# GpSimd adds epsilon and makes ScalarE's shift in all layer norms of a decoder kernel, with another hand-written order and another table of constant matmuls

## The chip, the cores and the metric

The kernel runs on one core of one Trainium2 chip. Its engines are TensorE (PE in the profile, with its weight loads as PEld), VectorE (DVE), ScalarE (ACT), GpSimd (POOL) and SyncE (SP), which issues the DMAs. They run their own instruction streams and meet at semaphores. The metric is the device time of one execution in microseconds; lower is better.

## The reference

Four sequences of 512 tokens with 256 channels go through two decoder layers. Each of the six sublayers is added to its input and a layer norm follows it:

```python
def _layernorm(x, axis=-1, eps=1e-05):
    m = jnp.mean(x, axis=axis, keepdims=True)
    v = jnp.var(x, axis=axis, keepdims=True)
    return (x - m) / jnp.sqrt(v + eps)

x = _layernorm(x + _L0_attn_ref(x, ...))        # causal softmax attention
x = _layernorm(x + _L0_xattn_ref(x, ctx, ...))  # masked cross attention, with a norm of its own inside
x = _layernorm(x + _L0_ffn_ref(x, ...))         # three layers of +1/-1 weights
x = _layernorm(x + _L1_attn_ref(x, ...))        # performer: causal linear attention, 16 heads
x = _layernorm(x + _L1_xattn_ref(x, ctx, ...))  # mLSTM: gated attention, 8 heads, group norm
x = _layernorm(x + _L1_ffn_ref(x, ...))         # quantized: rounded tokens and weights, conv of 3 taps
```

## The kernel before

**Streams.** The four sequences go as two streams, a (`first`) and b (`second`), in two rounds (n = 0, 1). Each stream has its own tiles and four of the eight PSUM banks, and both share the engines. A sequence is four tiles of 128 tokens (t = 0 to 3); most steps handle a pair p of them. The stages are called self, cross, sign, perf, mlstm and quant in the code; the first four are the front half.

**The order.** For each engine there is one generator for each stream that yields the name of a section ("sign.xT0") before it issues it. `weave` runs them by the strings in `TURNS`: "a12 b1 a6" is twelve sections of stream a, one of b, six of a. So the order on each engine is written out by hand, and an engine that waits for one stream doesn't pass to the other. Stream b runs behind a by about half a round.

**Constant matmuls.** At the head of many PE sections stands `claim`. It waits until the PSUM bank is free, and then issues as many 128x512 bf16 matmuls of constants into it as `KEEP` has for "section stream round" (line 558), 162 in all at 71 places. The result is overwritten. Only after them does PE wait for the operands of the section's own work.

**The norm of a pair.** `stats` on VectorE takes bn_stats of both tiles (L1181), bn_aggr (L1184), and adds EPS to the variances into `rstd` (L1187), which signals `var_in`. `rstd` on GpSimd raises that to the power -0.5 (L2116) and signals `rstd_made`. `normalize` on VectorE then makes the shift -mean*rstd of the pair (L1193), signals `shift_made`, and subtracts and multiplies the even tile (L1196). `normalize` on ScalarE waits for `shift_made` and makes the odd tile as rstd*x + shift (L1789). What follows, transposes on PE (L565) for instance, waits for both tiles. There are 56 such pairs; 8 of them are of the norm inside cross attention (i = 1), which has no shift and no ScalarE tile: there `spread_by_gamma` reads the mean and `add_residual` the rstd. At the very end the last normalized tiles are stored.

Line 1742 is the last scaling in quant (eight of 0.69 us to a pass), 2200 GpSimd's power in the mLSTM's group norm, 572 the projections, 1090 the taps of the convolution, 807 and 821 the performer's features, 1053 and 1042 the mLSTM's outputs.

## Time and profile before

| | |
|---|---|
| median of 3 runs | 794.84 us (794.0 to 796.28) |
| the profiled execution, its own time | 796.56 us |
| its span from the first to the last instruction | 795.2 us |
| outside the span | 1.36 us |
| instructions | 14785 |
| busy PE, DVE, ACT, POOL | 737.0, 572.7, 330.0, 183.3 us |
| granted TensorE clock, mean over the span | 0.985 |
| constant matmuls (L558) | 162 |

The profiled execution is 1.72 us above the median of the runs. Durations below come from it. A matmul's busy time overlaps that of the one behind it, since they are pipelined, so PE time is read as the distance from start to start: four constant matmuls take 0.88 us from the first start to the start of what follows, 0.22 us each.

### The profile page before, as it was taken

The numbers are of one execution on the slowest core, as the hardware profiler recorded it, in microseconds if no ns is written. First come the engines' busy times: TensorE is split into PE (matmuls) and PEld (weight loads), VectorE is DVE, ScalarE is ACT, GpSimd is POOL, SyncE is SP. The second block draws the span as 40 slices with busy tenths as digits, with TensorE's granted clock in tenths as the row PEclk, the third lists the DMA queues.
The fourth block names the chain that finished last, engine by engine and source line by source line (L and its number), as shares of the span: only waits on it lengthen the run. The fifth ranks groups of instructions, "written<-read, shape, count | busy, mean of one in ns | idle before, by whom it ended". The sixth has DMA issues, their size and how long they took to land.

```text
span 795.2 us, 14785 instructions
## 1 busy us (share of the span) xinstructions
PE 737.0 (93%) x5962; PEld 478.7 (60%) x5962; DVE 572.7 (72%) x1388; ACT 330.0 (42%) x608; POOL 183.3 (23%) x277
## 2 busy tenths in 40 slices
PE   9999999999999988899989999999999998998494
PEld 5778455667657655567654475857646585646232
DVE  1558745576476788988998963857656578799886
ACT  2576313323153226475338534241333413286253
POOL 8711000610015320022441020112204412012300
PEclk9999999999999999999999999999999999999698
DMA  9503000100011000041100030000000000000001
GB/s 349 194 2 133 0 1 1 54 2 2 1 28 28 27 2 2 1 120 42 27 2 1 0 107 1 2 1 3 1 1 1 1 2 2 1 2 1 0 1 53
DMA packets 12739, 23.76 MB, mean 30 GB/s; under 512 B 768, under 2 KB 7040, under 8 KB 12416
## 3 DMA queue, kind: packets, MB, share of 16 engines
q1 hardware_dynamic: 12672, 22.82, 8.3%
q8 instruction: 47, 0.77, 0.4%
q14 instruction: 20, 0.16, 0.1%
HBM read 20.72 MB, written 2.10 MB: 29 GB/s over the span
## 4 chain that ended last, share of the span: by engine, by line
PE 65%; DVE 18%; issue 8%; ACT 7%; POOL 2%; DVEq 0%; ACTq 0%; POOLq 0%
PE bank L762 8%; PE bank L580 6%; PE bank L572 6%; PE bank L627 5%; PE bank L606 4%; PE bank L856 4%; PE bank L772 3%; PE bank L1090 3%; PE bank L748 2%; PE bank L841 2%; PE bank L807 2%; DVE work L1474 2%; PE bank L866 1%; DVE stats L1181 1%; PE bank L710 1%
## 5 line engine op out<-in xcount | busy, mean ns | idle before, releaser
L2116 POOL TENSOR_TENSOR rstd<-rstd,minus_half 128x2 f32<-128x2 f32 x56 | 41.9, 748 | 434.3 <-DVE rstd L1187 434.0
L762 PE MATMUL bank<-work,f0w 128*128 128x512 f16 x512 | 114.2, 379 | 0.0
L762 PEld LDWEIGHTS bank<-work,f0w 128*128 128x128 f16 x512 | 49.4, 98 | 59.5 <-issue 1.9
L1904 ACT ACTIVATE work<-bank 128x512 f16<-128x512 f32 x64 | 37.1, 595 | 68.8 <-PE bank L762 47.7
L1392 DVE SCALAR_TENSOR_TENSOR work<-bank,work 128x512 f16<-128x512 f32 x64 | 43.0, 686 | 22.2 <-ACT work L1904 22.1
L558 PE MATMUL bank<-bar_upper,identb 128*128 128x512 bf16 x162 | 48.0, 389 | 4.9 <-DVE work L1474 2.0
L627 PE MATMUL bank<-work 128*128 128x256 f32 x208 | 50.6, 382 | 0.5 <-ACT work L1833 0.5
L1474 DVE TENSOR_TENSOR work<-bank,upper 128x512 f32<-128x512 f32 x64 | 41.3, 685 | 12.3 <-PE bank L856 12.0
L627 PEld LDWEIGHTS bank<-work 128*128 128x128 f32 x208 | 37.3, 190 | 5.8 <-ACT work L1833 1.0
L1257 DVE TENSOR_REDUCE small<-bank 128x1 f32<-128x512 f32 (+3 forms) x32 | 18.8, 587 | 30.0 <-PE bank L608 30.0
L2200 POOL TENSOR_TENSOR small<-small,minus_half 128x16 f32<-128x16 f32 x8 | 24.0, 3004 | 63.8 <-DVE small L1632 63.8
L856 PE MATMUL bank<-work 64*128 64x128 f32 x512 | 37.2, 285 | 1.6 <-DVE work L1456 0.9
L1181 DVE BATCH_NORM_STATS2 stats<-y 128x6 f32<-128x256 f32 x96 | 36.2, 414 | 3.0 <-ACT y L1882 2.9
L856 PEld LDWEIGHTS bank<-work 64*128 64x128 f32 x512 | 31.1, 187 | 11.2 <-issue 4.6
L572 PE MATMUL bank<-xT,perf_w 128*128 128x512 f32 x64 | 30.9, 615 | 1.5 <-ACT work L1929 0.6
L1929 ACT ACTIVATE work<-bank 128x512 f32<-128x512 f32 x40 | 21.2, 596 | 26.4 <-PE bank L807 26.4
L1818 ACT ACTIVATE work<-bank,small 128x512 f32<-128x512 f32 (+3 forms) x32 | 19.4, 606 | 27.4 <-DVE small L1261 19.8
L606 PE MATMUL bank<-ctxT,work 128*128 128x512 f32 x64 | 30.6, 600 | 0.0
L1090 PE MATMUL bank<-work,f0w 128*128 128x512 f32 x64 | 30.2, 595 | 0.4 <-DVE work L1695 0.4
L1569 DVE TENSOR_TENSOR work<-work 128x512 f32<-128x512 f32 x32 | 24.5, 787 | 6.6 <-ACT work L1990 6.3
L772 PE MATMUL bank<-f0w,work 128*128 128x256 f16 x256 | 29.3, 273 | 0.0
L558 PEld LDWEIGHTS bank<-bar_upper,identb 128*128 128x128 bf16 x162 | 15.0, 101 | 21.9 <-issue 5.2
(306 smaller groups left out, 1654.9 us busy)
## 6 DMA issues: line engine op xcount, KB each, us to landing
work<-in_mask SPq DMA_DIRECT2D x4, 1024.0 KB, 7.0
xT<-in_xT SPq DMA_DIRECT2D x4, 512.0 KB, 4.2
ctxT<-in_ctxT SPq DMA_DIRECT2D x4, 512.0 KB, 5.7
perf_w<-in_k SPq DMA_DIRECT2D x3, 512.0 KB, 11.7
perf_w<-in_perf_w SPq DMA_DIRECT2D x1, 1536.0 KB, 6.1
x<-in_x SPq DMA_DIRECT2D x2, 512.0 KB, 11.0
ctx<-in_w SPq DMA_DIRECT2D x2, 512.0 KB, 13.8
work<-in_w SPq DMA_DIRECT2D x1, 1024.0 KB, 16.1
```

Of the source, the lines that this page charges most:

```text
L558: nc.tensor.matmul(u.bank[:, :], identb[:, :], bar_upper[:, :, :].rearrange("p a b -> p (a b)"), start=True, stop=True)
L572: ins = nc.tensor.matmul(u.bank[:, :], weights[:, k, c0:c0 + P], src[:, k, :], start=(k == 0), stop=(k == NC - 1))
L580: ins = nc.tensor.matmul(u.bank[:, j * C:(j + 1) * C], src[:, k, t * P:(t + 1) * P], weights[:, k, c0:c0 + C], start=(k == 0), stop=(k == ...
L606: nc.tensor.matmul(u.bank[:, 0:width], s.a_qT[:, k, t * P:(t + 1) * P], keys[:, k, 0:width], start=(k == 0), stop=False)
L627: ins = nc.tensor.matmul(u.bank[:, 0:C], s.probT[:, t % 2, j * P:(j + 1) * P], v[:, j, :], start=(j == 0), stop=(j == tiles - 1))
L762: ins = nc.tensor.matmul(u.bank[:, :], f0w1[:, k, m * P:(m + 1) * P], s.h1[part][:, k, :], start=(k == 0 and part == 0), stop=(k == NF - 1 ...
L772: ins = nc.tensor.matmul(u.bank[:, 0:C], s.h2[part][:, k, t * P:(t + 1) * P], f0w2[:, k, :], start=(k == 0 and part == 0), stop=(k == NF - ...
L856: ins = nc.tensor.matmul(u.bank[:, here], s.kf[rows, pair, here], s.qf[rows, pair, here], start=True, stop=True, tile_position=(PM * i, 0))
L1090: ins = nc.tensor.matmul(u.bank[:, :], taps[:, j, k, :], s.flat[j % 4][:, k:k + T], start=(k == 0), stop=(k == 1))
L1181: m = vec.mark(nc.vector.bn_stats(s.stats[:, t, :], src[:, t, :]))
L1392: low_part(what, m, dst, number + m, lambda o, x, hi: nc.vector.scalar_tensor_tensor(out=o, in0=x, scalar=0.0, in1=hi, op0=ALU.max, op1=AL ...
L1474: nc.vector.tensor_tensor(s.inner[:, r % 4, :].rearrange("p (t q) -> p t q", t=NT), u.bank[:, :].rearrange("p (t q) -> p t q", t=NT), uppe ...
```

## The change

1. VectorE no longer adds EPS. The second bn_aggr signals `var_in` itself, and VectorE doesn't wait for the aggregates any more. GpSimd adds EPS from `mv` into `rstd`, waits for that, and takes the power.
2. VectorE no longer makes the shift. GpSimd makes it after the power, for the odd tile alone (one column), and signals `shift_made`; not in the norm i = 1.
3. `spread_by_gamma`, which relied on the wait that is gone, waits for `var_in`.
4. `TURNS` is another order on PE, DVE, ACT and POOL (SP's is the same), and `KEEP` is another table: 126 constants at 61 places.

```diff
 TURNS = {
     "tensor":
-        "a12 b1 a6 b1 a1 b1 a1 b1 a13 b4 a1 b3 p1 a2 b4 a3 b1 a7 b1 a19 b1 a2 b1 a2 b1 a1 b1 a1 b2 a1 b1 a1 b2 a1 b3 "
...
+        "a11 b1 a7 b1 a2 b2 a8 b1 a5 b4 a1 b4 p1 a2 b2 a3 b1 a5 b1 a11 b1 a5 b1 a4 b2 a1 b1 a2 b2 a1 b1 a1 b1 a1 b1 "
...
 KEEP = {
-    "quant.hidden5 0 0": 4, "quant.hidden6 0 0": 4, "quant.topT 0 0": 4, "quant.row2 0 0": 4, "self.q 0 1": 1,
...
+    "quant.turn0 0 0": 1, "quant.hidden1 0 0": 1, "quant.hidden3 0 0": 1, "quant.hidden4 0 0": 3,
...
         def stats(s, n, i, src, ready, p, name):
...
             dve.wait_ge(*m)
-            for t in (2 * p, 2 * p + 1):
-                m = vec.mark(nc.vector.bn_aggr(s.mv[:, t, :], s.stats[:, t, :]))
-            dve.wait_ge(*m)
-            two = slice(2 * p, 2 * p + 2)
-            nc.vector.tensor_scalar(s.rstd[:, two], s.mv[:, two, 1], EPS, None, ALU.add).then_inc(s.var_in.sem, 1)
+            vec.mark(nc.vector.bn_aggr(s.mv[:, 2 * p, :], s.stats[:, 2 * p, :]))
+            nc.vector.bn_aggr(s.mv[:, 2 * p + 1, :], s.stats[:, 2 * p + 1, :]).then_inc(s.var_in.sem, 1)

         def normalize(s, n, i, src, dst, p, name):
...
             dve.wait_ge(*s.rstd_made.at(n, s.place[i, p]))
-            nc.vector.scalar_tensor_tensor(out=s.shift[:, two], in0=s.mv[:, two, 0], scalar=-1.0, in1=s.rstd[:, two],
-                                           op0=ALU.mult, op1=ALU.mult).then_inc(s.shift_made.sem, 1)
             t = 2 * p
...
             def spread_by_gamma(p):

                 yield f"cross.in_norm{p}"
+                dve.wait_ge(*s.var_in.at(n, s.place[1, p]))
...
             yield f"{name}rstd{p}"
             pool.wait_ge(*s.var_in.at(n, s.place[i, p]))
             two = slice(2 * p, 2 * p + 2)
+            m = gps.mark(nc.gpsimd.tensor_scalar(s.rstd[:, two], s.mv[:, two, 1], EPS, None, ALU.add))
+            pool.wait_ge(*m)
             nc.gpsimd.tensor_tensor(s.rstd[:, two], s.rstd[:, two], minus_half[:, 0:2], ALU.pow).then_inc(s.rstd_made.sem, 1)
+            if i != 1:
+                pool.wait_ge(*s.rstd_made.at(n, s.place[i, p]))
+                t = 2 * p + 1
+                nc.gpsimd.tensor_scalar(s.shift[:, t:t + 1], s.mv[:, t, 0:1], -1.0, s.rstd[:, t:t + 1], ALU.mult,
+                                        ALU.mult).then_inc(s.shift_made.sem, 1)
```

Line numbers of the changed kernel are 2 lower than before up to `stats`, 7 and then 6 lower behind it, and 1 higher behind `rstd` on GpSimd. In the rows that follow, stretches of the program as they stand before and now are shown, without times.

**Place A: GpSimd, near the end, stream b's mLSTM.** Before: the six weighings of keys, the two powers of the group norm, and the powers of the two norm pairs; then the edges of the convolution.

```order
L2120 TENSOR_TENSOR ctx<-ctx,rows_all 128x256 x4
L2193 TENSOR_TENSOR work<-x,small 128x256 x6
L2200 TENSOR_TENSOR small<-small,minus_half 128x16 x2
L2116 TENSOR_TENSOR rstd<-rstd,minus_half 128x2 x2
L2206 MEMSET work 128x1
```

Now:

```order
L2121 TENSOR_TENSOR ctx<-ctx,rows_all 128x256 x4
L2194 TENSOR_TENSOR work<-x,small 128x256 x6
L2201 TENSOR_TENSOR small<-small,minus_half 128x16 x2
L2110 TENSOR_SCALAR rstd<-mv 128x2
L2112 TENSOR_TENSOR rstd<-rstd,minus_half 128x2
L2116 TENSOR_SCALAR shift<-mv,rstd 128x1
```

Each norm's power now has the addition ahead of it and the shift behind it (the second pair's three follow in the same way); the order of the rest is the same.

**Place B: VectorE, the same norm (its second pair).** L1742 (now L1736) is a scaling of stream a's quant, L1196 (now L1189) the even tile of the norm, L1663 (now L1657) the search for each token's largest value, which waits for both tiles. Before:

```order
L1181 BN_STATS stats<-y 128x6 x2
L1184 BN_AGGR mv<-stats 128x2 x2
L1187 TENSOR_SCALAR rstd<-mv 128x2
L1742 TENSOR_TENSOR work<-work,bank 128x512
L1193 SCALAR_TENSOR_TENSOR shift<-mv,rstd 128x2
L1196 TENSOR_SCALAR ctx<-y,mv,rstd 128x256
L1663 TENSOR_REDUCE small<-ctx 128x2
```

Now:

```order
L1179 BN_STATS stats<-y 128x6 x2
L1181 BN_AGGR mv<-stats 128x2
L1182 BN_AGGR mv<-stats 128x2
L1736 TENSOR_TENSOR work<-work,bank 128x512 x2
L1189 TENSOR_SCALAR ctx<-y,mv,rstd 128x256
L1657 TENSOR_REDUCE small<-ctx 128x2
```

The addition and the shift are gone, and between the aggregates and the even tile stand two scalings of the other stream in place of one. Ahead of the mLSTM's ratios, further up in the program, four of those scalings stand now, five before.

**Place C: TensorE, second round, stream b's second half of the performer features** (L807 queries and keys, L821 keys turned; 805 and 819 now) **beside stream a's mLSTM outputs** (L1042 and L1053; 1040 and 1051 now). L558 (now L556) are the constants. Before:

```order
L925 MATMUL bank<-work,head_spread 128x128 x4
L558 MATMUL bank<-bar_upper,identb 128x512 x4
L807 MATMUL bank<-work,perf_w 128x512 x4
L558 MATMUL bank<-bar_upper,identb 128x512 x4
L807 MATMUL bank<-work,perf_w 128x512 x4
L558 MATMUL bank<-bar_upper,identb 128x512 x4
L821 MATMUL bank<-perf_w,work 128x128 x12
```

Now:

```order
L805 MATMUL bank<-work,perf_w 128x512 x4
L556 MATMUL bank<-bar_upper,identb 128x512
L1040 MATMUL bank<-work,xT 128x132 x2
L556 MATMUL bank<-bar_upper,identb 128x512
L1051 MATMUL bank<-memory_back,work 128x132 x2
L1040 MATMUL bank<-work,xT 128x132 x2
L805 MATMUL bank<-work,perf_w 128x512 x4
L556 MATMUL bank<-bar_upper,identb 128x512 x2
L1051 MATMUL bank<-memory_back,work 128x132 x2
L819 MATMUL bank<-perf_w,work 128x128 x12
```

The same features have four constants ahead of and between them in place of twelve, and work of the other stream stands there.

## Rows read from the trace of the kernel before

**Rows 1.** The page: busy time by engine; the granted clock in 40 slices.

```profile
PE 737.0 (93%) x5962; PEld 478.7 (60%) x5962; DVE 572.7 (72%) x1388; ACT 330.0 (42%) x608; POOL 183.3 (23%) x277
...
PEclk9999999999999999999999999999999999999698
```

**Rows 2.** The page: the chain that ended last, by engine.

```profile
PE 65%; DVE 18%; issue 8%; ACT 7%; POOL 2%; DVEq 0%; ACTq 0%; POOLq 0%
```

**Rows 3.** Busy time by stretch: length, then each engine with instructions; clock; DMA; GB/s.

```profile
265.00:300.00 35.00, 30.02 (x368) 18.99 (x366) 29.85 (x74) 8.90 (x16) 12.04 (x21) 1.00 0.05 16
300.00:345.00 45.00, 38.48 (x426) 24.59 (x429) 42.64 (x85) 25.49 (x43) 4.17 (x6) 1.00 0.02 3
```

**Rows 4.** Groups of instructions: busy us, mean ns; idle before, what ended it.

```profile
L558 PE MATMUL bank<-bar_upper,identb 128*128 128x512 bf16 x162 | 48.0, 389 | 4.9 <-DVE work L1474 2.0 <-ACT work L1929 1.7 <-ACT work L1925 1.1
...
L1193 DVE SCALAR_TENSOR_TENSOR shift<-mv,rstd 128x2 f32<-128x2 f32 x48 | 12.1, 252 | 14.3 <-POOL rstd L2116 14.1
L1187 DVE TENSOR_SCALAR rstd<-mv 128x2 f32<-128x2 f32 x56 | 10.1, 180 | 1.9
...
L2116 POOL TENSOR_TENSOR rstd<-rstd,minus_half 128x2 f32<-128x2 f32 x56 | 41.9, 748 | 434.3 <-DVE rstd L1187 434.0
```

**Rows 5.** Timeline of PE: start, us, engine, line; constants and what follows them.

```profile
38.21 0.38 PE L558 MATMUL bank<-bar_upper,identb 128*128 128x512 bf16 x1
38.42 0.49 PE L565 MATMUL bank<-ident,x 128*128 128x128 f32 x3
...
722.34 0.59 PE L558 MATMUL bank<-bar_upper,identb 128*128 128x512 bf16 x2
722.77 0.38 PE L1001 MATMUL bank<-parts,head_row 128*128 128x512 bf16 x1
```

**Rows 6.** Timeline of PE at place C; in brackets idle before, what ended it.

```profile
656.39 1.03 PE L558 MATMUL bank<-bar_upper,identb 128*128 128x512 bf16 x4
...
660.12 1.04 PE L558 MATMUL bank<-bar_upper,identb 128*128 128x512 bf16 x4 [1.02 <-ACT work L1929]
...
662.92 1.04 PE L558 MATMUL bank<-bar_upper,identb 128*128 128x512 bf16 x4 [0.64 <-ACT work L1929]
```

**Rows 7.** Timeline of a norm pair that nothing delays (sign, stream a, first round).

```profile
117.78 0.25 DVE L1184 BATCH_NORM_AGGREGATE mv<-stats 128x2 f32<-128x6 f32 x2
118.06 0.17 DVE L1187 TENSOR_SCALAR rstd<-mv 128x2 f32<-128x2 f32 x1
...
118.31 0.69 POOL L2116 TENSOR_TENSOR rstd<-rstd,minus_half 128x2 f32<-128x2 f32 x1 [26.51 <-DVE rstd L1187]
...
119.04 0.16 DVE L1193 SCALAR_TENSOR_TENSOR shift<-mv,rstd 128x2 f32<-128x2 f32 x1 [0.25 <-POOL rstd L2116]
119.24 0.60 ACT L1789 ACTIVATE x<-y,shift,rstd 128x256 f32<-128x256 f32 x1 [5.64 <-DVE shift L1193]
```

**Rows 8.** Small instructions on GpSimd: two groups, and one in the timeline.

```profile
L2135 POOL TENSOR_SCALAR small<-small 128x32 f32<-128x32 f32 x4 | 1.6, 409 | 0.3
...
L2206 POOL MEMSET work<- 128x1 f32 x16 | 1.2, 98 | 2.7 <-DVE ctx L1196 1.6 <-DVE x L1196 1.1
...
145.82 0.30 POOL L2135 TENSOR_SCALAR small<-small 128x32 f32<-128x32 f32 x1
```

**Rows 9.** Timeline of a norm pair whose VectorE part comes late (cross, stream b).

```profile
161.90 0.70 POOL L2116 TENSOR_TENSOR rstd<-rstd,minus_half 128x2 f32<-128x2 f32 x1 [6.54 <-DVE rstd L1187]
...
165.59 0.60 ACT L1789 ACTIVATE x<-y,shift,rstd 128x256 f32<-128x256 f32 x1 [1.84 <-DVE shift L1193]
```

**Rows 10.** Timeline: a GpSimd addition and a VectorE shift at the same time.

```profile
415.51 1.28 POOL L2132 TENSOR_TENSOR work<-x 128x512 f32<-128x512 f32 x1
...
415.52 1.29 DVE L1193 SCALAR_TENSOR_TENSOR shift<-mv,rstd 128x2 f32<-128x2 f32 x1 [0.22 <-POOL rstd L2116]
```

**Rows 11.** Timeline of GpSimd at place A: the group norm's power and the next.

```profile
740.46 3.29 POOL L2200 TENSOR_TENSOR small<-small,minus_half 128x16 f32<-128x16 f32 x1 [1.03 <-DVE small L1632]
...
743.71 0.69 POOL L2116 TENSOR_TENSOR rstd<-rstd,minus_half 128x2 f32<-128x2 f32 x1
```

More of the change, by code:

```diff
@@ L38 @@
     "tensor":
[8 rows of a table removed]
-    "vector":
[11 rows of a table removed]
-    "scalar":
[6 rows of a table removed]
[8 rows of a table added]
+    "vector":
[11 rows of a table added]
+    "scalar":
[7 rows of a table added]
     "gpsimd":
-        "a7 b2 a5 b1 a1 b4 a5 b3 a1 b1 a2 b2 a2 b4 a2 b1 a2 b4 a3 b1 a4 b1 a2 b1 a1 b1 a1 b1 a1 b6 a2 b1 a1 b1 w1 b2 "
-        "a1 b1 a4 b1 a1 b9 a2 b2",
+        "a7 b2 a5 b4 a1 b1 a5 b5 a3 b1 a1 b1 a1 b3 a2 b1 a2 b5 a10 b2 a1 b5 a1 b2 a2 b3 w1 b3 a3 b1 a4 b9 a2 b2",
     "sync":
```

75 rows, old and new, of tables (KEEP, TURNS) are left out of this document.

## The prediction, made before the changed kernel had run

> **What bounds the kernel now.** I read the page first. TensorE is busy for 93% of the span, and its granted clock is the upper of its two levels, 2.4 GHz, nearly everywhere; the one slice marked 6 lies near the end, at 736 to 755 us [rows 1]. The chain that ended last is PE for 65% and VectorE for 18%, with 2% for GpSimd [rows 2]. So TensorE is the bound over most of the program, and VectorE shares that place in some stretches: from 265 to 345 us it is busy for 72.5 of 80 us, more than PE's 68.5 [rows 3]. But 162 of PE's matmuls are constants [rows 4] that compute nothing. At 0.22 us from start to start they hold 35 us of its time. They stand ahead of a wait, and whether they cost anything depends on whether the wait outlasts them. I went through the 71 places in the timeline. At 28 of them, with 54 constants, the work behind starts 0.21 to 0.23 us after the last constant's start and without idle time, as at the first and the last of them [rows 5]: no wait is left there, and in the worst case all of it is lost. At the other 43 a wait is still seen behind or ahead of them, and the constants mostly fill time that would be idle anyway. The 56 norm pairs lie between: each holds up only its own stream, and PE mostly has the other stream's work meanwhile.
>
> **The norm pair.** Today a pair with nothing in its way takes, from the end of the second aggregate (117.78 + 0.25) to the start of ScalarE's tile (119.24), 1.21 us: 0.03 to the addition, 0.17 for it, 0.08 to GpSimd, 0.70 for the power, 0.03 to the shift, 0.16 for it, 0.04 to ScalarE [rows 7]. The changed pair is 0.08 to GpSimd, the addition, a wait on itself, 0.70, a wait on itself, the shift, 0.04. The wait between two dependent GpSimd instructions is 0.3 us over four, so 0.08 [rows 8]. An addition over 2 columns on GpSimd is nowhere in the trace. From below it is bounded by a memset of one column, 0.10 us, and from above by the tensor_scalar over 32 columns, 0.30 us in an undisturbed place and 0.41 in the mean of four [rows 8]. I take 0.22 for it and for the shift: the instruction is of the kind of the dearer row, and its size is that of the cheaper one. That makes 0.08 + 0.22 + 0.08 + 0.70 + 0.08 + 0.22 + 0.04 = 1.42 us, 0.21 more than today. With 0.10 it is 1.18 (0.03 less), with 0.41 it is 1.80 (0.59 more). Moving small work to GpSimd doesn't shorten the chain in itself.
>
> It does so where VectorE is late. At 161.90 the power took 0.70 us and ended at 162.60, but ScalarE's tile started at 165.59 [rows 9], since the shift stood in VectorE's queue behind other work. 23 of the 48 shifts begin over 0.3 us after their power. There ScalarE gets free to start before VectorE's own tile, and the pair ends with VectorE's tile of 0.41 us, not with the shift, the hop and ScalarE's 0.60: about 0.38 us earlier. PE stands at the result of a norm pair at about a dozen of the 48, prompt and late ones mixed. Six times +0.21 and six times -0.38 is -1.0 us. Against that stand the last norms, which nothing covers. In the mLSTM near the end GpSimd ends the group norm's power at 743.75 and goes to the next at once [rows 11]; the addition, which VectorE made meanwhile, now comes behind it: +0.30. The last pair before the store is prompt: +0.21. At place B two scalings of 0.69 stand before the even tile in place of one, though one fewer stands ahead of the ratios, which evens out; and the rest of the mLSTM's and quant's prompt pairs in that stretch add about 1 us. I put the whole at **+0.5 us**, and between -2 and +9 (below).
>
> **What VectorE gets back.** The additions are busy for 10.1 us and the shifts for 12.1 [rows 4], 22.2 in all. The shifts' mean of 0.252 against 0.16 when prompt is contention: one took 1.29 us exactly beside a GpSimd addition of 1.28 us [rows 10]. The Trainium skill (GPSIMD Engine Reference, section 8, Key points) says that GpSimd shares its SBUF interfaces with VectorE, and that they contend when the VectorE instruction has two SBUF inputs; the rows agree, and by it the shift loses this stall when GpSimd itself makes it. The 22.2 us count only where VectorE is the bound: 0 if nowhere, 18% of them, 4.0 us, if by its share of the chain [rows 2]. I take the stretch of rows 3: 4 of the 56 pairs lie in it, so 22.2 x 4 / 56 = **-1.6 us**. The new wait in `spread_by_gamma` is on an aggregate right ahead of it, and it takes the place of the wait for the addition: nothing.
>
> **What PE gets back.** The table has 36 constants fewer, 7.9 us at 0.22. By place: the 28 places without a wait go from 54 to 27, 5.9 us less of paid time. The 43 others go from 108 to 59, and 40 constants stand at 25 new places. What the new ones cost is not known. If, as before, a third of them (54 of 162) is paid in full, they take 40 / 3 x 0.22 = 2.9 us. Ends: 8.8 if all are paid, 0 if all fill waits. Net **-3.0 us**. Of the covering ones that go, place C is where something better comes in. There twelve constants stand in three groups with 1.02 and 0.64 us of idle time ahead of two of them [rows 6], and now the other stream's mLSTM outputs stand there, with four constants. The eight that go are real work's time: **-1.8 us**, between 0 and the 1.8 + 1.66 of constants and idle time together. At the other covering places idle time takes the constants' place, at no cost, unless the clock falls. All groups there are of at most four, so 0.9 us, and idle time of that length was there before at full clock (1.02 us in rows 6); I count nothing.
>
> **Sum.** +0.5 - 1.6 - 3.0 - 1.8 = -5.9 us. Made against the profiled execution, that is 796.56 - 5.9 = 790.7 (795.2 of span before, 1.36 around it). That execution was 1.72 above the median, so the median of runs would be 794.84 - 5.9 = **788.9 us**. SP's order is untouched, and the DMAs before the last store are hidden.
>
> **Rivals.**
> *The waits stay (same).* PE's place is set by VectorE and ScalarE at the covering places, so fewer constants only become idle time; all 40 new ones are paid (8.8), against 5.9 that goes: +2.9. Place C gives 1.8, VectorE 1.6, and the norms cost 0.5: 794.8 us. For it speaks that at 43 of 71 places a wait outlasts the constants. Against it: the order was changed with the table, and waits move too.
> *More comes back.* The new constants all fill waits (-5.9), place C -1.8, VectorE by its share of the chain -4.0, norms at +0.5: -11.2, 783.6 us. For it speaks that VectorE is busier than PE for 80 us; against it, that GpSimd adds nothing to a prompt chain.
> *GpSimd's chain is the new bound (slower).* If both small instructions take 0.41 us, the mean with contention in rows 8, every prompt pair gets 0.59 us longer. The sign turns the sign once the pairs on the path number over 6.4 / 0.59 = 11, with -1.6 - 3.0 - 1.8 = -6.4 standing against them. With 16 on the path, in the chains of rounds' ends and of quant, it is +9.4 - 6.4 = +3.0, 797.8 us, and with the additions behind long GpSimd work (3.29 us in rows 11) up to 800. For it: 25 of 48 pairs are prompt today, and GpSimd's queue gets 104 more instructions, with a VectorE instruction of two inputs able to hold each up. Against it: PE has the other stream's work at most of them. The Trainium skill (GPSIMD Engine Reference, section 3.1, Elementwise) has the same direction: VectorE stays the engine for elementwise work. No row here shows a pair made in the new way.
> *The change doesn't free VectorE.* Two aggregates take 0.25 us, one about 0.17 [rows 7], so small instructions already overlap, and the freed slots may hold little; and if GpSimd's 104 new instructions stall VectorE as its addition did in rows 10, -1.6 becomes +1 or so, 791.5 us, inside the forecast's own range.
>
> **How the numbers follow.** Forecast 0.44 (own range 785.5 to 792.4), waits stay 0.17, more comes back 0.13, slower 0.23, not freed 0.03. A measurement of this kernel can tell about 0.3% from no change, which is 792.5 to 797.2. Faster: 0.44 + 0.13 + 0.03 = 0.60. Same is the case of the waits, 0.17. Slower is 0.23. The range 782.5 to 799 takes in all cases' centres, the unknown price of the small instructions and of the new constants, and leaves out the low tail of one and the high tail of the other, some 15%.
>
> **What would show it.** Steps right: L556 counts 126, and the start-to-start sum of constants falls from 35 to about 27 us; few constants directly followed by work without idle; GpSimd's addition and shift at 0.2 to 0.25 us in the median; a prompt pair at 1.4 us from aggregate to ScalarE's tile; VectorE's busy time down by some 20 us; place C without idle ahead of L805 and L819; the stretch that is now 265 to 345 us shorter by 2 us or more. Wrong: small GpSimd instructions of 0.4 us and more, PE idle at the transposes (L563, L1069) growing by several us, the granted clock falling at a place where constants are gone, or a longer stretch from stream b's last gate to the end, which takes 96 us now.

## The result, and the profile after

| | before | after |
|---|---|---|
| median of runs | 795.88 us (7 runs, 794.0 to 796.88) | 791.44 us (7 runs, 790.51 to 792.93) |
| ratio, 95% interval | | 0.9948 (0.9934 to 0.9962) |
| the profiled execution | 796.56 us, span 795.2 | 790.51 us, span 789.2 |
| busy PE, DVE, ACT, POOL | 737.0, 572.7, 330.0, 183.3 us | 728.3, 550.6, 330.8, 218.7 us |
| constants, from start to start | 162, 35.6 us | 126, 27.6 us |

The change makes the kernel 0.5% faster, 4.1 us (3.0 to 5.2), where 5.9 were forecast. The two profiled executions differ by 6.0 us, but that of before is one of its slower ones and that of after its fastest, so the traces overstate the gain by 1.9 us. Differences in us below are ratios times 795.

The page of after, its busy times and its granted clock; [rows 1] has those of before:

```profile
PE 728.3 (92%) x5926; PEld 476.3 (60%) x5926; DVE 550.6 (70%) x1284; ACT 330.8 (42%) x608; POOL 218.7 (28%) x381
...
PEclk9999999999999999999999999999999999999796
```

The groups that answer to [rows 4]. L2110 is GpSimd's new addition, L2116 its shift:

```profile
L2110 POOL TENSOR_SCALAR rstd<-mv 128x2 f32<-128x2 f32 x56 | 14.9, 267 | 397.1 <-DVE mv L1182 396.5
...
L556 PE MATMUL bank<-bar_upper,identb 128*128 128x512 bf16 x126 | 38.3, 389 | 5.2 <-DVE work L1468 2.5 <-ACT work L1919 1.4 <-ACT work L1923 0.6
L2112 POOL TENSOR_TENSOR rstd<-rstd,minus_half 128x2 f32<-128x2 f32 x56 | 40.5, 722 | 4.7
L2116 POOL TENSOR_SCALAR shift<-mv,rstd 128x1 f32<-128x1 f32 x48 | 17.2, 358 | 5.1
```

The timeline of the pair of [rows 7] in after, all three engines, and last the shift of the next pair:

```profile
122.48 0.18 DVE L1181 BATCH_NORM_AGGREGATE mv<-stats 128x2 f32<-128x6 f32 x1
122.58 0.15 DVE L1182 BATCH_NORM_AGGREGATE mv<-stats 128x2 f32<-128x6 f32 x1
...
122.81 0.22 POOL L2110 TENSOR_SCALAR rstd<-mv 128x2 f32<-128x2 f32 x1 [31.15 <-DVE mv L1182]
123.11 0.71 POOL L2112 TENSOR_TENSOR rstd<-rstd,minus_half 128x2 f32<-128x2 f32 x1
123.86 0.41 DVE L1189 TENSOR_SCALAR x<-y,mv,rstd 128x256 f32<-128x256 f32 x1 [0.76 <-POOL rstd L2112]
123.93 0.39 POOL L2116 TENSOR_SCALAR shift<-mv,rstd 128x1 f32<-128x1 f32 x1
...
124.36 0.60 ACT L1783 ACTIVATE x<-y,shift,rstd 128x256 f32<-128x256 f32 x1 [6.26 <-POOL shift L2116]
...
126.83 0.26 POOL L2116 TENSOR_SCALAR shift<-mv,rstd 128x1 f32<-128x1 f32 x1
```

From the end of the second aggregate (122.73) to ScalarE's tile (124.36) are 1.63 us, against 1.21. The addition takes the 0.22 us of the forecast. The shift takes 0.39 us here and 0.26 at 126.83, and the rows tell why: here VectorE's even tile runs from 123.86 to 124.27, and the shift ends 0.05 us behind it; there VectorE is idle. Of the 48 shifts 33 overlap the even tile. The 30 that begin behind its start took 0.39 to 0.43 us, and the 3 that begin ahead of it 0.26; of the 15 that don't overlap it 13 took 0.26. The freed VectorE now starts its tile just when GpSimd wants to make the shift. The Trainium skill (SBUF — State Buffer, Who interferes with whom) lists VectorE's `tensor_scalar` among the instructions that can enter a mode that takes the port pair shared with GpSimd, and says that the second to come then waits for the first to end. The order of starts agrees (0.39 us behind the tile, 0.26 ahead of it); which mode the tile ran in, no row shows.

**Where the time went.** I added up TensorE's own work (every matmul but the constants, each at the median distance to the next of its kind) and read when both kernels had done the same amount. The table has a row where the difference turns:

| own work done, us | before at | after at | difference |
|---|---|---|---|
| 20 | 25.2 | 24.5 | -0.7 |
| 40 | 46.1 | 47.6 | +1.5 |
| 200 | 229.5 | 231.6 | +2.1 |
| 280 | 359.4 | 358.4 | -1.0 |
| 360 | 453.5 | 451.5 | -2.0 |
| 480 | 592.9 | 588.4 | -4.5 |
| 520 | 642.3 | 638.8 | -3.5 |
| 540 | 683.9 | 677.2 | -6.7 |
| 560 | 710.3 | 702.7 | -7.6 |
| all | 795.2 | 789.2 | -6.0 |

Three places stand out: a loss of 2.2 us at 40 us, a gain of 3.1 between 230 and 359 us, and one of 3.2 at place C (638.8 to 677.2). The two orders do different work at the same amount, so a single row can be off by some us; at place C the rows of the two traces below give the same 3.2. Two more differences, a gain of 2.5 us between 453 and 593 us and a loss of 1.6 behind 710 us, no row here explains.

The loss is this, PE in after, and the granted clock there (by stretch: length; busy us and instructions of PE, PEld, DVE, ACT, POOL; clock; DMA; GB/s):

```profile
38.16 0.63 PE L563 MATMUL bank<-ident,x 128*128 128x128 f32 x4 [1.26 <-ACT x L1783]
38.63 5.30 PE L578 MATMUL bank<-wv,xT 128*128 128x256 f32 x16
...
36.00:40.00 4.00, 2.74 (x19) 2.49 (x19) 1.91 (x7) 2.58 (x3) 2.24 (x6) 0.94 0.00 0
40.00:44.00 4.00, 4.00 (x14) 3.24 (x13) 2.06 (x10) 3.25 (x8) 0.27 (x1) 0.63 0.01 2
```

In before [rows 5] the transposes at 38.42 followed their one constant without a wait. Here PE waits 1.26 us for ScalarE's tile of the first norm pair, and at 39.52 its clock falls to 1.2 GHz for 3.41 us; the 16 matmuls behind take 5.30 us, where before they took 3.62. In both kernels GpSimd comes to this pair only at 35.8 us, when its long work at the start ends. In before the power alone was left to it and ScalarE's tile began at 36.77; now the addition and the slower shift are too, and it begins at 37.42.

Before had such a fall as well, in the second round, and the prediction didn't see it: behind a wait of 0.81 us, also at transposes of normalized tiles, its clock is at the lower level for 3.41 us from 614.76.

```profile
613.83 0.63 PE L565 MATMUL bank<-ident,ctx 128*128 128x128 f32 x4 [0.81 <-DVE ctx L1196]
...
612.00:616.00 4.00, 3.08 (x26) 2.12 (x26) 2.99 (x9) 2.36 (x6) 4.00 (x8) 0.85 0.02 4
```

Place C in after, PE; [rows 6] show it before:

```profile
648.51 1.14 PE L805 MATMUL bank<-work,perf_w 32*128 32x512 f32 x8 [0.50 <-DVE y L1482]
649.59 0.39 PE L556 MATMUL bank<-bar_upper,identb 128*128 128x512 bf16 x1
...
650.26 0.38 PE L556 MATMUL bank<-bar_upper,identb 128*128 128x512 bf16 x1
...
651.69 1.14 PE L805 MATMUL bank<-work,perf_w 32*128 32x512 f32 x8 [0.15 <-issue]
652.77 0.60 PE L556 MATMUL bank<-bar_upper,identb 128*128 128x512 bf16 x2
...
654.34 0.95 PE L819 MATMUL bank<-perf_w,work 32*128 32x128 f32 x24 [0.52 <-DVE work L1435]
```

Idle time and constants come to 0.50 + 0.22 + 0.22 + 0.15 + 0.44 + 0.52 = 2.1 us. Before they were 1.57 from 656.39 to the first projection, 1.02 + 1.02 ahead of the second and 0.64 + 0.97 ahead of the turned keys, 5.2 us: 3.2 less.

### The profile page after: what moved, and what is told of

Read it like the earlier page. It is cut to its first block, busy times and chain, and to the rows that moved or that the text cites. A ratio compares the mean times of both kernels' runs of the same rounds, so it can differ in the third digit from the quotient of the medians.

```text
span 789.2 us, 14720 instructions
## 1 busy us (share of the span) xinstructions
PE 728.3 (92%) x5926; PEld 476.3 (60%) x5926; DVE 550.6 (70%) x1284; ACT 330.8 (42%) x608; POOL 218.7 (28%) x381
## 4 chain that ended last, share of the span: by engine, by line
PE 30%; DVE 10%; ACT 4%; POOL 4%; issue 2%; DVEq 0%; POOLq 0%
PE bank L760 7%; PE bank L570 2%; PE bank L854 2%; PE bank L1088 2%; PE bank L770 2%; PE bank L578 2%; PE bank L604 1%; PE bank L625 1%; PE bank L746 1%; DVE work L1736 1%; PE bank L839 1%; POOL f0w L2223 1%; PE bank L864 1%; DVE stats L1179 1%; DVE work L1563 1%
## 5 line engine op out<-in xcount | busy, mean ns | idle before, releaser
L2110 POOL TENSOR_SCALAR rstd<-mv 128x2 f32<-128x2 f32 x56 | 14.9, 267 | 397.1 <-DVE mv L1182 396.5
L556 PE MATMUL bank<-bar_upper,identb 128*128 128x512 bf16 x126 | 38.3, 389 | 5.2 <-DVE work L1468 2.5
L1563 DVE TENSOR_TENSOR work<-work 128x512 f32<-128x512 f32 x32 | 24.5, 784 | 5.1 <-ACT work L1984 5.1
```

What stands on the lines that cost most here:

```text
L556: nc.tensor.matmul(u.bank[:, :], identb[:, :], bar_upper[:, :, :].rearrange("p a b -> p (a b)"), start=True, stop=True)
```

## The experiments

**The two halves apart.** `e1_order` has the norms of before with the order and table of after, `e2_norms` the reverse. The norm part of `e1_order` against after:

```diff
-            nc.vector.bn_aggr(s.mv[:, 2 * p + 1, :], s.stats[:, 2 * p + 1, :]).then_inc(s.var_in.sem, 1)
...
+            dve.wait_ge(*m)
+            two = slice(2 * p, 2 * p + 2)
+            nc.vector.tensor_scalar(s.rstd[:, two], s.mv[:, two, 1], EPS, None, ALU.add).then_inc(s.var_in.sem, 1)
...
-            m = gps.mark(nc.gpsimd.tensor_scalar(s.rstd[:, two], s.mv[:, two, 1], EPS, None, ALU.add))
...
-                nc.gpsimd.tensor_scalar(s.shift[:, t:t + 1], s.mv[:, t, 0:1], -1.0, s.rstd[:, t:t + 1], ALU.mult,
...
```

> The norms as before (VectorE adds epsilon and makes the shift of the pair), the order and the table of constants of after. Theory A, the gain is the order's and the table's: this alone is at 790 to 792 us, as fast as after or faster, because a prompt pair then reaches ScalarE's tile in 1.21 us and not in 1.63. Theory B, the gain is VectorE's freed 22 us: this alone is at 795 us or above, since 104 small instructions are back on VectorE in an order that was written for their absence. The granted clock tells a third thing: if the wait of 1.26 us for ScalarE's tile at 36.9 us is the slow pair's, it is shorter here (0.6 us or so) and the clock doesn't fall at 39.5 us.

> The norms of after, the order and the table of constants of before. Theory A: 796 to 799 us; a prompt pair is 0.42 us longer, and PE stands at the result of some of them; what VectorE gets back is hidden. Theory B: 792 to 793 us, or better, with VectorE's waits shorter at the stretch from 265 to 345 us. If neither part alone gives anything (both this and the order alone at 795 or above), the two belong together: the order is of use only with GpSimd's norm.

Measured: the order alone 0.9973 (0.9964 to 0.9982), 2.1 us faster than before; the norms alone 1.0021 (1.0009 to 1.0034), 1.7 us slower. Together they are 4.1 us faster, so 3.7 us belong to neither (the three intervals together leave about 1.7 either way): the order is of most use with the norms that it was written for, and those are a loss in the old one. Under the new order the norms are worth 2.0 us (0.9973 against 0.9948, and the intervals don't touch). For the norms alone theory A holds; the order alone lies between its two theories. In `e1_order` the wait at 37 us is 0.45 us, and the clock doesn't fall there, as expected.

**What a pair's latency is worth.** `e6_add_twice` repeats GpSimd's addition:

```diff
             m = gps.mark(nc.gpsimd.tensor_scalar(s.rstd[:, two], s.mv[:, two, 1], EPS, None, ALU.add))
             pool.wait_ge(*m)
+            m = gps.mark(nc.gpsimd.tensor_scalar(s.rstd[:, two], s.mv[:, two, 1], EPS, None, ALU.add))
+            pool.wait_ge(*m)
```

> After, with GpSimd's addition of epsilon made twice in each of the 56 pairs (0.22 us and 0.09 of wait on itself): every pair gets 0.31 us longer, and VectorE, ScalarE and TensorE have the work that they had. It measures what the latency of a pair is worth. Theory A, the prediction's count: PE stands at a dozen pairs, so 12 x 0.31 = 3.7 us more than after, 795 us. Theory B, the other stream's work covers nearly all of them: under 1 us, 792.4 or less. Theory C, the pairs are the bound: 25 or more of them count, 7.8 us and more, 799 us.

Measured: 1.0062 (1.0047 to 1.0078), 9.1 us above after: theory C. Followed weight load by weight load the profiled execution falls 11 us behind that of after, in steps of 0.3 to 0.7 us that mostly stand at transposes of normalized tiles, and in 3.2 us of two more falls of the clock (407.5 and 424.6 us). Without those some 8 us are left, as much as about 25 pairs of 0.31 us and not a dozen. That is a price and not a count: PE's waits ahead of the transposes of line 563 grew by 3.3 us (2.7 to 6.0), the rest lies elsewhere. The added instructions also hold GpSimd for 17 us, and no run tells a longer pair from a busier GpSimd. Here is one of the places, PE first in after, where the transposes of both pairs run without a wait:

```profile
220.65 1.04 PE L563 MATMUL bank<-ident,x 128*128 128x128 f32 x8
```

and in `e6_add_twice`, where the second half of them waits for ScalarE's tile:

```profile
222.34 0.60 PE L563 MATMUL bank<-ident,x 128*128 128x128 f32 x4
223.34 0.63 PE L563 MATMUL bank<-ident,x 128*128 128x128 f32 x4 [0.40 <-ACT x L1783]
```

In after PE comes to these transposes just as the tiles are there. So a trace with no wait at a norm doesn't show that the norm has time to spare.

**Each of the two moves undone.** Both kernels have the order and table of after.

> After, with the shift of the pair back on VectorE (epsilon stays on GpSimd; the order and the table of after). A prompt pair is 0.08 + 0.22 + 0.10 + 0.71 + 0.03 + 0.16 + 0.04 = 1.34 us to ScalarE's tile, 0.29 less than in after, but the shift is in VectorE's queue again. Theory A, the prompt pairs' latency is what counts: 790 us or less. Theory B, the gain of after comes from ScalarE no longer standing behind VectorE's queue, where the sum of all waits of ScalarE's tiles fell from 166 to 114 us: 793 us or more.

> After, with epsilon added by VectorE again and the shift on GpSimd (the order and the table of after). A prompt pair is 0.03 + 0.17 + 0.08 + 0.70 + 0.10 + 0.39 + 0.04 = 1.51 us, 0.12 less than in after, and the addition no longer stands behind long GpSimd work: the first pair (GpSimd busy until 35.8 us) reaches ScalarE 0.31 us earlier and the last pair of the mLSTM too. VectorE gets 10 us of additions back. Theory A, latency: 790.5 to 791 us. Theory B, VectorE's time: 10 us x 18% of the chain = 1.8 us more, 793 us. The granted clock: with PE idle for about 0.95 us at 37 us in place of 1.26, the fall at 39.5 us is seen if it takes that little, and not seen if it takes more.

```diff
             dve.wait_ge(*s.rstd_made.at(n, s.place[i, p]))
+            nc.vector.scalar_tensor_tensor(out=s.shift[:, two], in0=s.mv[:, two, 0], scalar=-1.0, in1=s.rstd[:, two],
+                                           op0=ALU.mult, op1=ALU.mult).then_inc(s.shift_made.sem, 1)
```

(`e7_shift_on_vector`; `e8_add_on_vector` has VectorE's wait and addition of before in `stats` instead.) Measured: 0.9967 (0.9955 to 0.9979) and 0.9964 (0.9953 to 0.9975), 1.5 and 1.3 us above after, with overlapping intervals in both. Theory B names 793 us for both; the 792.4 and 792.1 are nearer to it than to theory A. Each makes a prompt pair shorter and neither is faster: less latency than the order was written for gives nothing visible, where more costs. Their profiled executions also have falls of the clock at 38.3 and 38.5 us and at 403.5 and 420.8.

**VectorE's time by itself.**

> After, with VectorE making the pair's addition of epsilon and its shift as well, behind its even tile of the pair and into a scratch tile that nobody reads: its queue has the work of before again (about 104 small instructions, 15 to 20 us busy), and no pair waits for them. It measures the freed time of VectorE by itself. Theory A, the prediction's term: 1.6 us above after, 793.0 us. Theory B, by VectorE's share of the chain (18%) or more: 4 us above, 795.4 us. Theory C, it is hidden: 791.4 us.

```diff
             nc.vector.tensor_scalar(dst[:, t, :], src[:, t, :], s.mv[:, t, 0:1], s.rstd[:, t:t + 1],
                                     ALU.subtract, ALU.mult).then_inc(s.normed_v.sem, 1)
+            nc.vector.tensor_scalar(scrap[:, 4 * p:4 * p + 2], s.mv[:, two, 1], EPS, None, ALU.add)
+            nc.vector.scalar_tensor_tensor(out=scrap[:, 4 * p + 2:4 * p + 4], in0=s.mv[:, two, 0], scalar=-1.0,
+                                           in1=s.rstd[:, two], op0=ALU.mult, op1=ALU.mult)
```

Measured: 0.9977 (0.9965 to 0.9988), 2.3 us above after. The groups of the added instructions in `e12_vector_busy`:

```profile
L1192 DVE TENSOR_SCALAR scrap<-mv 128x2 f32<-128x2 f32 x48 | 8.4, 175 | 0.0
...
L1193 DVE SCALAR_TENSOR_TENSOR scrap<-mv,rstd 128x2 f32<-128x2 f32 x48 | 7.5, 156 | 0.0
```

They are 15.9 us by their own durations, and 7.7 of the engine's busy time (550.6 to 558.3), since they overlap their neighbours. So the run gives back only a part of the 22.1 us that VectorE lost. The result is nearest to theory A (the two intervals leave about 1.4 us either way). It isn't the clock alone: five of the 12 runs, with mean clocks of 0.980 to 0.981, took 792.4 to 792.6 us, and after took 791.1 to 791.4 at 0.979.

But the time isn't lost where theory A, the prediction's term, has it. That term was worked out for the stretch from 265 to 345 us. From stream b's first performer transposes to the start of stream a's last layer of quant, PE needs 95.18 us in before (247.10 to 342.28) and 92.68 in after (249.21 to 341.89). These are the same two places, first in `e12_vector_busy`, with the added work, and then in `e1_order`, with all of VectorE's work of before:

```profile
249.66 0.63 PE L564 MATMUL bank<-ident,x 128*128 128x128 f32 x4
...
342.49 0.94 PE L1139 MATMUL bank<-f1w,work 128*128 128x256 bf16 x7
```

```profile
248.45 0.63 PE L563 MATMUL bank<-ident,x 128*128 128x128 f32 x4
...
341.24 0.94 PE L1138 MATMUL bank<-f1w,work 128*128 128x256 bf16 x7
```

That is 92.83 and 92.79 us, as in after, while `e2_norms`, the new norms in the old order, has 94.80 (247.26 to 342.06). So the 2.5 us of this stretch are the order's and the table's. Matched weight load by weight load, the profiled execution of `e12_vector_busy` is 0.6 us behind after at 343 us, 2.9 at 423 and 3.6 at the end; in between, at 403.67, it has a fall of the clock for 3.41 us (1.7 us of work) that the one of after doesn't have.

**The constants.** `e4_before_fewer` is before without 50 constants at 28 places. It isn't quite the prediction's list of 28 places with 54 constants: three of those places, with 9 constants, keep them, and three others, with 5, lose them.

> Before, without the 50 constants at 28 places where the work behind them starts with no wait left. Theory A, the working of the prediction taken to its end (such a constant is paid in full): 50 x 0.22 = 11 us less, 784 to 785 us. Theory B, PE's place is set by the other engines at the next wait, which takes the time back: 794 to 796 us, with as much more idle time as constants are gone. Between them, a price of one such constant as the time gained over 50. Theory C: the granted clock falls at places where constants are gone, and the time is above 796 us.

```diff
 KEEP = {
-    "quant.hidden5 0 0": 4, "quant.hidden6 0 0": 4, "quant.hidden6 0 1": 4, "quant.hidden7 0 1": 4,
-    "mlstm.head1 1 1": 4,
...
```

Measured: 1.001 (0.9998 to 1.0022): 0.8 us slower, if anything. In the profiled execution 50 x 0.22 = 10.9 us of constants are gone, and the span is only 2.4 shorter (792.8), so 0.05 us a constant; the rest has become idle time and slower matmuls. Even that is an upper end, since this execution is the fastest of its 12 (794.19) and that of before one of the slower (796.56, where the median beside these runs is 794.96): between the medians nothing came back. The stretches near its end, first of `e4_before_fewer`, then of before:

```profile
700.00:720.00 20.00, 15.96 (x125) 8.52 (x126) 18.29 (x30) 18.48 (x29) 1.74 (x3) 0.91 0.00 1
720.00:740.00 20.00, 14.59 (x155) 11.72 (x155) 19.01 (x44) 8.05 (x15) 7.93 (x6) 0.84 0.01 2
```

```profile
700.00:720.00 20.00, 19.15 (x144) 9.46 (x140) 18.65 (x30) 17.47 (x26) 2.27 (x3) 1.00 0.00 1
720.00:740.00 20.00, 15.23 (x169) 11.90 (x169) 17.98 (x40) 9.98 (x20) 7.78 (x7) 1.00 0.00 1
```

VectorE's 18 to 19 us of 20 bound both. Before filled the rest of PE's time with constants and kept 2.4 GHz; without them PE was 16.0 us busy in place of 19.2 and the clock fell at 709.4 and 719.7. Over its 12 runs the time follows the mean clock: 0.980 goes with 794.2 to 794.4 us, 0.977 with 797.4 to 798.0. That is theories B and C at once.

`e11_old_table` puts the table of before under the order of after:

> After with the table of constants of before (162 in place of 126; norms and order of after). It measures what the table alone is worth under the new order. Theory A, as the prediction had it, a constant at a place without a wait is paid: 3 us and more above after, 794.5 us or above. Theory B, as e4_before_fewer showed (50 constants, 2.4 us of span): 36 constants make 1.8 us at most, 793 us or less. Theory C, many of the old places have no wait now: 57 unpaid ones and more, 5 us above after, 796 us.

Measured: 1.0034 (1.0019 to 1.0049), 6.8 us above after, with falls of the clock at 38, 311 and 407 us in the profiled execution: the time of theory C, but not its reason. By the prediction's rule (the work behind starts 0.21 to 0.23 us after the last constant) 65 constants stand without a wait in it and 66 in after, so their number isn't what costs; nor is the clock, since its 12 runs have the mean clock of after, 0.979. Where the constants stand makes the difference, and a table is fitted to one order; which of the places cost it, no run shows. I have no run with the new table under the old order.

**The clock.** `e3_cover` and `e10_best` put constants where after is idle:

> After, with four constants at the transposes of the first normalized pair (stream a, first round, start of cross attention), where before had one and after has none. In after PE is idle for 1.26 us there, and 1.4 us later its granted clock falls to the lower level for 3.41 us, in which it does half the work. Theory A, that idle time brings the fall: here PE is busy with constants through it, the clock stays at the upper level, and the time falls by half of 3.41 us, 1.7 us, to about 789.7 us (ratio to before 0.993). Theory B, the fall has another cause or only moves: 791.4 us or more, and a fall of the clock is seen at another place of the first 100 us.

> After, with other constants in the last 20 us: twelve at stream b's last transposes of largest values and six at the row of token scales, where PE is idle for 3.2 and 1.6 us and has one each, and none ahead of the last layer of quant, where it has three that run at the lower clock and take 1.73 us. Theory A: the clock stays up from 770 to 777 us, the two groups of transposes on the path take 0.6 in place of 1.1 us each, so 1.0 us less than after, 790.4 us; the three constants that go cost nothing, since what follows waits for ScalarE's cast (0.24 us of idle time behind them). Theory B, the three were paid: up to 1.7 us less besides, 788.7 us. Theory C: the new constants don't keep the clock, or hold the transposes up: 791.4 or more.

> After with the constants of the last 20 us as in e9_tail, and with enough of them for the whole of two waits further up: eight at the first normalized pair's transposes (four left 0.93 us of idle time, and the clock fell all the same) and twelve at stream b's first turn of rounded tokens, where after has one and 2.49 us of idle time, and where e3_cover, e8_add_on_vector and e9_tail fell to the lower clock at 402 to 404 us. Theory A, idle time brings these falls: none of the two is seen, each gives back half of 3.41 us, and the time is 1.7 to 3 us under e9_tail's, 787 to 788 us (ratio to before 0.990 to 0.991). Theory B, the falls come in spite of full cover: 789.7 us, as e9_tail.

```diff
 KEEP = {
...
-    "quant.turn0 1 0": 1, "quant.topT 1 1": 1, "quant.row2 1 1": 1, "quant.down0 1 1": 3
+    "quant.turn0 1 0": 12, "quant.topT 1 1": 12, "quant.row2 1 1": 6, "cross.xT0 0 0": 8
```

This is `e10_best`. `e3_cover` has only the last entry, with 4; `e9_tail` has only `topT`, `row2` and `down0`.

Measured: `e3_cover` 0.9967 (0.9955 to 0.9979), no gain (1.5 us above after, with overlapping intervals); `e9_tail` 0.9935 (0.9918 to 0.9951), 1.0 us under after, though the intervals overlap; `e10_best` 0.9918 (0.9905 to 0.9931), 2.4 us under after and 6.5 under before. PE in `e3_cover` (one of the four constants has no record), with the stretch of the clock:

```profile
36.40 0.81 PE L556 MATMUL bank<-bar_upper,identb 128*128 128x512 bf16 x3
38.15 0.90 PE L563 MATMUL bank<-ident,x 128*128 128x128 f32 x4 [0.93 <-ACT x L1783]
...
36.00:40.00 4.00, 2.99 (x13) 2.19 (x15) 1.93 (x7) 2.60 (x3) 2.24 (x6) 0.80 0.00 0
```

and in `e10_best`:

```profile
36.81 1.89 PE L556 MATMUL bank<-bar_upper,identb 128*128 128x512 bf16 x8
38.53 0.60 PE L563 MATMUL bank<-ident,x 128*128 128x128 f32 x4
38.97 3.62 PE L578 MATMUL bank<-wv,xT 128*128 128x256 f32 x16
...
36.00:40.00 4.00, 4.00 (x26) 2.99 (x26) 1.86 (x7) 2.54 (x3) 2.24 (x6) 1.00 0.00 0
```

Four constants left 0.93 us idle, and the clock fell at 38.36; eight left none, it stayed, and the 16 matmuls take 3.62 us again. They hold the transposes up to 38.53, 0.4 us later than in after. But `e9_tail`, which has no constants here, shows the wait without the fall:

```profile
38.21 0.63 PE L562 MATMUL bank<-ident,x 128*128 128x128 f32 x4 [1.04 <-ACT x L1782]
...
36.00:40.00 4.00, 2.96 (x22) 2.75 (x22) 1.86 (x7) 2.54 (x3) 2.25 (x6) 1.00 0.00 0
```

So the wait doesn't bring the fall each time. Each of the 14 kernels has one profiled execution. In eight of them PE is idle for 0.93 to 1.93 us at this place, and the clock falls behind it in seven; in six the idle time is 0.45 us or none, and it falls in none. At the wait of 2.49 us ahead of stream b's turn the fall comes in some executions and not in others. The clock there in after, then in `e3_cover`, both with PE 1.51 us busy from 400 to 404:

```profile
400.00:404.00 4.00, 1.51 (x13) 0.96 (x12) 3.86 (x12) 1.82 (x6) 2.25 (x4) 1.00 0.00 0
404.00:408.00 4.00, 4.00 (x20) 3.24 (x19) 3.90 (x15) 1.66 (x3) 0.93 (x2) 1.00 0.00 0
```

```profile
400.00:404.00 4.00, 1.51 (x12) 0.96 (x11) 3.86 (x12) 1.75 (x5) 2.19 (x4) 0.95 0.00 0
404.00:408.00 4.00, 4.00 (x13) 2.97 (x12) 3.90 (x14) 1.03 (x3) 0.93 (x2) 0.62 0.00 0
```

With twelve constants there `e10_best` shows no fall, and its four runs lie within 0.6 us (788.77 to 789.37), where the seven of after spread over 2.4. At the end of the program after has this, with the clock at 1.2 GHz:

```profile
770.40 1.11 PE L1110 MATMUL bank<-ident,work 128*128 128x128 f32 x4 [2.82 <-DVE work L1710]
771.30 0.63 PE L556 MATMUL bank<-bar_upper,identb 128*128 128x512 bf16 x1
772.91 1.12 PE L1058 MATMUL bank<-ident,small 128*128 128x128 f32 x4 [0.98 <-DVE small L1496]
```

and `e10_best` this:

```profile
770.11 0.66 PE L1110 MATMUL bank<-ident,work 128*128 128x128 f32 x4 [0.44 <-DVE work L1710]
770.60 1.46 PE L556 MATMUL bank<-bar_upper,identb 128*128 128x512 bf16 x6
772.17 0.65 PE L1058 MATMUL bank<-ident,small 128*128 128x128 f32 x4
774.34 4.60 PE L1128 MATMUL bank<-f1w,work 128*128 128x256 bf16 x24 [1.52 <-ACT work L2034]
```

The transposes that VectorE waits for take 0.66 us and not 1.11, which is theory A of `e9_tail`; what follows waits for ScalarE's cast by 1.52 us, so the three constants that went ahead of it had cost nothing. Not all of it is gain: the low clock that begins at 732 us lasts 17.07 us in this execution and 10.24 in that of after.

The last run takes 26 constants at places without a wait out of `e10_best`:

> e10_best without 26 constants at 18 places between 298 and 682 us where after starts the work behind them with no wait left (the places in the last 100 us stay, since taking such ones from before went with a lower clock there). With e11_old_table it prices a constant at a place without a wait in the new order. Theory A, it is paid there, as the 36 of e11_old_table cost 6.8 us over after: 26 x 0.19 = 5 us less than e10_best, 784 us. Theory B, the next wait takes the time back, as in e4_before_fewer: 26 x 0.05 = 1.3 us less, 788 us. Theory C, the clock falls where they are gone, at 0.0021 of mean clock and 1.7 us a fall: 789 us or more.

Measured: 0.9935 (0.9918 to 0.9952), 1.4 us above `e10_best`, with overlapping intervals. The clock fell at 417.4 and 775.8 in the profiled execution, and four of its six runs have a mean clock of 0.979 to 0.981, against 0.986 to 0.989 in `e10_best`: theory C. The other two, at 0.989, took 788.6 and 789.1 us, where the run of `e10_best` at 0.989 took 788.8: at the same clock the 26 constants cost nothing that can be seen. `e10_best` has the lowest ratio of all, and its interval (0.9905 to 0.9931) lies below that of after.

## Why the prediction was right, and where it wasn't

The forecast was -5.9 us from the case "faster", 788.9 us; the result is -4.1 and inside the range. The sign holds, and so does the main line, that the order and the table bring the gain and the new norms don't by a shorter chain. Of the terms only place C stands, and it gave more. That the sum comes within 1.8 us is partly luck, since the errors of the others cancel:

- **VectorE, -1.6.** Its busy time fell by 22.1 us as forecast. `e12_vector_busy` costs 2.3 us, part of it clock, so the size is about right. The step to it isn't: it took VectorE as the bound from 265 to 345 us and counted the pairs there. That stretch is 2.5 us shorter, which was the mark for the term, but it is so with VectorE's old work too (92.8 us in `e1_order` and `e12_vector_busy`, 92.7 in after). The mark came true for another reason.
- **Place C, -1.8.** 3.2 us, near the ceiling of 3.5 that the term had: the idle time ahead of the projections went too, since the other stream's work lies in it.
- **PE's constants, -3.0.** This step failed, twice. It took a third of the 40 new ones, 13, as standing without a wait, and 27 at the old places. By its own rule it is 28 of the new ones and 38 at old places: 54 at 28 places before, 66 at 35 now, since places that had a wait have lost it. So the step's own arithmetic gives 12 x 0.22 = +2.6 us and not -3.0. And such a constant isn't paid in full: at most 0.05 of 0.22 us in `e4_before_fewer`, and nothing that can be seen at equal clock in `e13_lean`. "No wait behind it" means that the wait comes later, not that there is none. The table as a whole does matter, by 6.8 us in `e11_old_table`, with as many constants without a wait.
- **The clock, 0.** "I count nothing" was the missing term. It took the 1.02 us of idle time at full clock in [rows 6] as the measure for all places, though before itself has a fall behind 0.81 us at 613.8. At 38 us a wait of 1.26 us cost 3.41 us at half clock, 1.7 us of PE's time, and 0.93 did too in `e3_cover`, while 0.45 in `e1_order`, 1.04 in `e9_tail` and 2.49 at 400 us in after didn't. `e10_best` gives back 2.4 us by constants alone, added at three places. The miss of 1.8 us is of this size; that it is exactly this, no run shows.
- **The norms, +0.5.** A sum of wrong terms. The addition took its 0.22 us, the shift 0.39 where the even tile runs and not 0.22, so a prompt pair is 1.63 us and not 1.42. A longer pair costs as if about 25 of them bore on the end and not a dozen (`e6_add_twice`). In stream b's mLSTM, place A, ScalarE's tile comes 2.61 us behind the aggregate and not 1.95: +0.66, where +0.30 stood. `e2_norms`, which holds VectorE's gain as well, is at +1.7 us. The late pairs gained: the 48 times from aggregate to ScalarE's tile sum to 114 us, before 166; 36 of the 52 are the two pairs of stream a's last norm, whose ScalarE tiles stood last in their part of the old order.
- **The sum.** The terms were added as if independent. The halves alone give -2.1 and +1.7, together -4.1: 3.7 us is in their fit to each other, and the prediction had no place for that. The norms are a loss in the old order and worth 2.0 us in the new one, so no single number could stand for them.

The rival of GpSimd's chain had a right core (a prompt pair is 0.42 us longer, and a longer pair costs more than thought), but the new order was written around the longer pair. The sign of failure "a longer stretch from stream b's last gate to the end" came true (96.2 to 98.4 us) and meant nothing: the order moved the gate forward. From stream a's last row of largest values (721.90, now 715.59) to the end it is 73.3 and 73.6 us. The sign "granted clock falling where constants are gone" came true and did matter. The sign "PE idle at the transposes growing by several us" came true in half: line 1069 has 4.1 us where before had 1.8, and line 563 has 2.7 where it had 3.4.

## What to carry to other kernels

In a kernel whose order is written by hand, price a change of one step's latency in the new order by lengthening that step a little and timing it: here 0.31 us on every norm pair cost 9 us, in part at places where the trace had no wait, and shortening gave nothing. Don't add up an order and the edits that it was written for as separate terms. Before you trim filler, look for TensorE waits with a fall of the granted clock behind them, fill those completely, and read several executions, since one alone may not show the fall. Filler ahead of work that could start was nearly free in two kernels here, where the next wait took its time back; a table from another order was not. And where a stretch gets shorter as forecast, ask a run with one half undone whether it did so for the forecast reason.

## What the runs showed of the hardware

- An addition over 128x2 fp32 on GpSimd takes 0.22 us, the one-column shift 0.26, and two dependent small instructions stand 0.08 to 0.11 us apart. Begun behind VectorE's 128x256 fp32 tile of 0.41 us the shift takes 0.39 and ends 0.05 us behind the tile; begun ahead of it, or beside VectorE's statistics of 0.41 us, it takes 0.26.
- Behind 0.93 to 1.93 us of TensorE idle time at one place of the program the granted clock fell for 3.41 us in 7 of 8 profiled executions, and behind 0.45 us or none in 0 of 6; at another place it fell behind 0.81 us.
- The same 2.49 us of TensorE idle time was followed by the lower clock in some executions and not in others, so one kernel has times in steps: after ran at 790.5, 791.1 to 791.4 and 792.8 to 792.9 us with mean clocks of 0.983, 0.979 and 0.977.
